# A vision tower on one core: the routed experts' last 64 features as pairs of 64-row matmuls

## The chip, the cores and the metric

The kernel runs on one core of one Trainium2 chip. The metric is the device time of one execution in microseconds (us), as the median of several runs.

## The reference

32 images of 38 tokens with 192 features pass through patch embedding, a selective scan, a layer of routed experts, a two-directional Mamba layer and a second mixture of experts. Each layer adds to a residual. The change lies in the first layer of routed experts alone, which is this, all in float32:

```python
B, S, H, F, E, TOP_K = (4, 512, 192, 768, 8, 2)
router_logits = jnp.einsum('th,eh->te', xf, Wr)
topk_vals, topk_idx = jax.lax.top_k(router_logits, TOP_K)
h = jnp.einsum('th,efh->etf', xf, Wi) + bi[:, None, :]     # wide: 192 -> 768
h = jax.nn.gelu(h, approximate=False)
expert_out = jnp.einsum('etf,ehf->eth', h, Wo) + bo[:, None, :]   # narrow: 768 -> 192
```

## The kernel before

The 32 images go through in four groups of 304 tokens. A first pass (`first`) holds the embedding, the first scan and the routing; a second pass (`part_a`, `part_b`) holds the Mamba scans and the second mixture. Each part has 12 steps, and the order of the work on each engine is written out by hand: five programs with semaphores between them.

The routed experts work on blocks of 128 token rows of one expert. There are 34 blocks, 0 to 33, each with its own expert's weights from DRAM. Blocks 0 to 4 (`SCAN_BLOCKS`) lie between the steps of the last group's first scan. Blocks 5 to 14 lie between the routing steps of the last group, 15 to 25 in the first `part_a`, and 26 to 33 in the first `part_b`, which have no scan yet (`IN_SCAN`, `IN_ROUTE`, `IN_PART_A`, `IN_PART_B`).

A block b passes through these steps:

- SP (`load_block`) fetches its 128 rows into XB, the wide weights into WX and WXR, and the narrow weights into WX and WXB. Three buffers rotate, so the fetches for block b wait for steps of block b - 3.
- `turn(b)` on TensorE (lines 1885 and 1886) transposes the rows: features 0 to 127 and features 64 to 191, into one PSUM bank (`SHARED_BANK`).
- `copy_x(b)` on VectorE (lines 1492 and 1493) copies them to XT: slot 0 holds features 0 to 127; slot 1 holds features 128 to 191 on partitions 64 to 127, and zeros on partitions 0 to 63. Then it signals `xt_copied`.
- `widen(b, halves)` makes the 768 hidden features as six tiles of 128, in two halves of three, each half in a PSUM bank. Each tile is two matmuls: the first 128 features (WX), and the last 64 (WXR, whose upper 64 rows are zeros, so it has 128 rows as well). One float32 matmul of the program is two MATMULs and two LDWEIGHTS in the trace, all on line 1670.
- `gelus(b)` on ScalarE (line 1008) makes HX from each half as it is signalled by `wide_mm`.
- `narrow(b)` multiplies HX by the narrow weights (12 MATMULs) into the same shared bank as the transposes. It waits for `xt_copied` of block b + 2, since VectorE reads that bank.
- `copy_y(b)` (line 1500) adds the bias, and GpSimd stores the rows.

TensorE's order in `experts(b)` from block 5 on is: first half of b, `turn(b + 1)`, second half of b, `narrow(b - 1)`. For blocks 0 to 4 it is `turn(b + 1)`, first half, `narrow(b - 1)`, second half. On VectorE each step ends with `copy_x(b + 1)` and `copy_y(b - 1)`.

The second pass starts behind the last blocks: SP waits for `mixed` of group 1 before it reads the scan's rows (line 510).

Of the kernel before, what the change touches and what calls it, by code (L numbers as in the profile page):

```python
# [6 lines left out]
BATCH, SEQ, D = 32, 38, 192  # L7
# [7 lines left out]
DM, DR = 128, 64  # L15
# [39 lines left out]
SCATTERS = 16 * (2 * TILES + 1)  # L55
M_CHAIN = 17
NBLK = 128

# [56 lines left out]
def vit_tower(nc, x_p, c128a, c64a, c128, c64, ex_m, ex_r, ex_b, out_m, out_r):  # L117
    fp32, bf16, i32, u32 = mybir.dt.float32, mybir.dt.bfloat16, mybir.dt.int32, mybir.dt.uint32
    ALU, ACT, AX = mybir.AluOpType, mybir.ActivationFunctionType, mybir.AxisListType
    with ExitStack() as ctx:  # L120
# [19 lines left out]
        negA = sb("negA", [128, 2 * FEAT_BLOCKS])  # L140

        WX = sb("WX", [128, 3, FFN + FT * D + FT])
        WXR = sb("WXR", [128, 3, FFN])
        WXB = sb("WXB", [128, 3, D])


# [113 lines left out]
        GATHERED = (GA0, GA0, GA, GA)  # L260
        passed = xp[0:TW, :, :].rearrange("p k t -> p (k t)")[:, 6 * D:6 * D + 2 * HALF_BLOCKS * EXPERTS].rearrange("p (a b e) -> p a b e", a=2, e=EXPERTS)
        XTOK = M.ACC
        ZERO = WXR[:, :, :].rearrange("p b n -> p (b n)")[:, 0:PLACES * D // 8]
        LZ = aP[:, 0, 1, :]
        DT24 = aP[0:RANK, 1, 1, 0:T]
        DT24K = aP[:, 1, 1, 0:T]
# [66 lines left out]

        negA_bounded, prep_pool, prep_act = sem("negA_bounded"), sem("prep_pool"), sem("prep_act")
        blank = sem("blank")
        BLANKS = 18

        def norm_signals(s, n, count):
            s.ln_mean, s.ln_var = sig(n + "_ln_mean", count), sig(n + "_ln_var", count)
# [141 lines left out]
        def _(sp):  # L481
# [8 lines left out]
                a, b = SEG64[i], SEG64[i + 1]  # L490
                sp.dma_start(CR[0:DR, a:b], c64[:, a:b]).then_inc(s_const[i], 16)
            sp.wait_ge(prep_pool, 2)
            zeros = slots_d.rearrange("(p j r) n -> p j (r n)", p=128, j=8)

            def write_first_rows(p):

# [22 lines left out]
            def first(s, p, m):  # L519
                if s is not None:  # L520
                    sp.wait_ge(P.rows_written.sem, P.rows_written.after(s, 96))
                for c in range(QSTEPS):
                    if c == 5:
                        if m is not None:
                            sp.wait_ge(scan_out.sem, scan_out.after(m, 1))
                            sp.dma_start(h_md[m], M.Hm[:, :]).then_inc(h_stored.sem, 16)
                            sp.dma_start(h_rd[m], M.Hr[:, :]).then_inc(h_stored.sem, 16)
                    if s is None and p is None and c in (0, 1, 6):
                        load_block(SCAN_BLOCKS + (0, 1, 6).index(c))
                    if c == 5:  # L530
                        if follows(p) is not None:
                            sp.wait_ge(tok_mm.sem, tok_mm.after(p, 2))
                            sp.dma_start(xp[:, :, :], x_p[p + 1]).then_inc(s_x, 16)
                    if c == 9 and p is not None:
                        write_first_rows(p)
                    if s is not None:
                        read_first_rows(s, c)
                    if s == 0 and c >= SLOTS:
                        sp.dma_start(zeros[:, c - SLOTS, :], ZERO).then_inc(s_zero, 16)
                    if s is not None and p is None:  # L540
                        if c == 4:
                            sp.wait_ge(table_ready, 1)
                            sp.wait_ge(c1_ready.sem, c1_ready.after(s, 1))
                            sp.wait_ge(base_ready.sem, base_ready.after(s, 1))
                        if c in (4, 5, 6):
                            load_wide(expert_of(c - 4), c - 4)
                        if c in (7, 8):
                            load_narrow(expert_of(c - 7), c - 7)
                        if c == 9:
                            sp.wait_ge(s_zero, 128)  # L550
                            sp.wait_ge(scattered.sem, scattered.after(PER_HALF, 0))
                        if c in (9, 10, 11):
                            load_rows(place_of(c - 9), c - 9)
                        if c == 11:
                            load_narrow(expert_of(2), 2)
                            load_block(3)
                            load_block(4)
# [6 lines left out]
            def load_wide(expert, p):  # L564

                sp.dma_start(WX[:, p, 0:WI], ex_m[bass.ds(expert, 1), :, 0:WI].rearrange("e p n -> p (e n)")).then_inc(s_wide[p], 16)
                sp.dma_start(WXR[DR:128, p, :], ex_r[bass.ds(expert, 1), :, :].rearrange("e p n -> p (e n)")).then_inc(s_wide[p], 16)

            def load_narrow(expert, p):

# [116 lines left out]
        def _(pool):  # L687
# [36 lines left out]
            def first(s, p, m):  # L724
                pieces = [(t, k) for t in range(TILES) for k in range(2)]
                for c in range(QSTEPS):
                    if s is not None:
                        if s == 0 and c == 0:
                            decay_step(0, 0)
                        if c + 1 < QSTEPS:  # L730
                            decay_step(s, c + 1)
                        elif p is not None:
                            decay_step(p, 0)
                        first_product(s, c)
                    if m and c in (1, 2, 3, 4):
                        scatter(m - 1, *pieces[c + 1])
                    if m and c == 6:
                        scatters_done(m - 1)
                    if m is not None and c == 10:
                        pool.wait_ge(s_zero, 128)  # L740
                        pool.wait_ge(xtok_copied.sem, xtok_copied.after(m, 2))
                        pool.wait_ge(slots_ready.sem, slots_ready.after(m, 1))
                        pool.sem_inc(turn_taken, 1)
                    if m is not None and c in (10, 11):
                        for t, k in (pieces[c - 10:c - 9] if s is not None else pieces if c == 10 else ()):
                            scatter(m, t, k)
                    if s is None and m is not None and c == 10:
                        pool.dma_start(keep_d[m], KEEP[:, :, :].rearrange("p t n -> p (t n)")).then_inc(scattered.sem, 16)
                    b = block_now(s, p, c)
                    if b is not None and b >= SCAN_BLOCKS:  # L750
                        if b == SCAN_BLOCKS:
                            for j in range(SCAN_BLOCKS - 2, SCAN_BLOCKS - 1):
                                store_block(j)
                        store_block(b - 1)
                    elif b is not None and b >= 2:
                        store_block(b - 2)
                if s is not None and m is not None:
                    pool.dma_start(keep_d[m], KEEP[:, :, :].rearrange("p t n -> p (t n)")).then_inc(scattered.sem, 16)
                if s is None and m is not None:
                    scatters_done(m)  # L760
# [381 lines left out]
        def _(dve):  # L1142
            for part in (CRA[DR:128, :], CR[DR:128, :], P.HrK[DR:128, :], P.XrK[DR:128, :], P.SQrK[DR:128, :], HIDrK[DR:128, :],
                         M.HrK[DR:128, :], M.XrK[DR:128, :], Q.SQrK[DR:128, :], M.LWK[:, :], M.gateK[:, :], M.ACCK[:, :],
                         Q.HrK[DR:128, :], Q.XrK[DR:128, :], Q.LWK[:, :], Q.gateK[:, :],
                         XT[0:DR, :, 1, :], HB[:, :]):
                nc.vector.memset(part, 0.0).then_inc(blank, 1)
            dve.wait_ge(blank, BLANKS)

# [337 lines left out]
            def copy_x(b):  # L1487
# [2 lines left out]
                if b >= 3:  # L1490
                    dve.wait_ge(wide_mm.sem, wide_mm.after(b - 3, 2))
                nc.vector.tensor_copy(XT[:, p, 0, :], PS[:, SHARED_BANK, 0:128])  # L1492
                nc.vector.tensor_copy(XT[DR:128, p, 1, :], PS[DR:128, SHARED_BANK, 128:256]).then_inc(xt_copied.sem, 1)  # L1493

            def copy_y(b):
                p = b % 3
# [167 lines left out]
        def _(pe):  # L1664
# [246 lines left out]
                else:  # L1911
                    pe.wait_ge(gelu_ready.sem, gelu_ready.after(HALF_BLOCKS + (q - 3) // 2, (q - 3) % 2 + 1))

            def widen(b, halves):
                p = b % 3
                if 0 in halves:
                    pe.wait_ge(xt_copied.sem, xt_copied.after(b, 1))
                    pe.wait_ge(s_wide[p], 32 * (b // 3) + 32)
                for h in halves:
                    bank_free(b, h)  # L1920
                    for j in range(HALF_FT):
                        out, f = PS[:, wide_bank(b, h), j * 128:(j + 1) * 128], h * HALF_FT + j
                        mm(out, WX[:, p, f * 128:(f + 1) * 128], XT[:, p, 0, :], True, False)
                        last = mm(out, WXR[:, p, f * 128:(f + 1) * 128], XT[:, p, 1, :], False, True)
                    last.then_inc(wide_mm.sem, 1)

            def narrow(b):
                p = b % 3
# [12 lines left out]
            def experts(b):  # L1941
# [3 lines left out]
                    return  # L1945
                if b < SCAN_BLOCKS:
                    turn(b + 1)
                    widen(b, (0,))
                    if b >= 1:
                        narrow(b - 1)  # L1950
                    widen(b, (1,))
                    return
                if b < BLOCKS:
                    widen(b, (0,))
                    if b + 1 < BLOCKS:
                        turn(b + 1)
                    widen(b, (1,))
                narrow(b - 1)

            def first(s, p, m):  # L1960
# [241 lines left out]
def _arrays(inp):  # L2202
# [66 lines left out]
    wo = I["L0_ffn_Wo"].reshape(EXPERTS, D, FT, 128).transpose(0, 3, 2, 1).reshape(EXPERTS, 128, FT * D)  # L2269
    bi = I["L0_ffn_bi"].reshape(EXPERTS, FT, 128).transpose(0, 2, 1)  # L2270
    ex_m = np.ascontiguousarray(np.concatenate([wi[:, 0:DM], bi, wo], axis=2))
    ex_r = np.ascontiguousarray(wi[:, DM:D])
    ex_b = np.ascontiguousarray(I["L0_ffn_bo"].reshape(EXPERTS, 1, D))
    b = "L1_attn_"
    put_both("down", I[b + "down_W"])
# [46 lines left out]
```

## Time and profile before

| | us |
|---|---|
| median of 3 runs | 959.54 |
| lowest and highest | 952.37, 961.0 |
| the profiled execution | 956.27 |
| its span, first to last instruction | 954.5 |

In the profile PE is TensorE's matmul side, PEld its weight loads, DVE is VectorE, ACT is ScalarE, POOL is GpSimd and SP the engine that issues most transfers. The mean granted clock of TensorE is 0.893 of full speed. PE is busy for 740.4 us of the span, DVE for 566.5, ACT for 404.1 and POOL for 394.6.

### The profile page before, as it was taken

Reading aid. Unit: us, or ns where it says so; the run is one execution under the profiler, and the core shown is the slowest. Engines: PE = TensorE matmul, PEld = TensorE weight load, DVE = VectorE, ACT = ScalarE, POOL = GpSimd, SP = SyncE. Lnnn points to the kernel's source line nnn. Section 1 sums busy time; section 2 is a strip of 40 time slices with the busy share of each in tenths; the row PEclk is TensorE's granted clock in tenths of the full one; section 3 lists DMA queues with packets and bytes.
Section 4 is the critical chain, followed back from the end, with each engine's and each line's share of the span. In section 5 each row is a group of like instructions: output and inputs, shape, how many; then the busy total and the mean of one; then the engine's idle time right before and its main releaser. Section 6 shows DMA issues by size and latency. Waiting matters only on the chain. (4 is left out here: it accounts for less than half of the span.)

```text
span 954.5 us, 11504 instructions
## 1 busy us (share of the span) xinstructions
PE 740.4 (78%) x3608; PEld 587.9 (62%) x3608; DVE 566.5 (59%) x968; ACT 404.1 (42%) x876; POOL 394.6 (41%) x311
## 2 busy tenths in 40 slices
PE   7977878586458879997999568777769885986756
PEld 5644656455327869997999356555556664764434
DVE  4167769679766532322112587988777787789320
ACT  1548275374134224332445446373617361733110
POOL 1045745655673311312013344544538333734503
PEclk9899899798678889999999789898979998997977
DMA  9469755355495567798786878697588657866221
GB/s 351 133 208 337 215 152 151 90 134 142 117 273 144 166 182 242 233 281 248 218 244 190 206 194 217 176 224 190 143 229 216 150 156 224 226 165 180 79 72 27
DMA packets 84668, 179.51 MB, mean 188 GB/s; under 512 B 12740, under 2 KB 32832, under 8 KB 83840
## 3 DMA queue, kind: packets, MB, share of 16 engines
q1 hardware_dynamic: 79776, 171.55, 64.1%
q0 software_dynamic: 4832, 7.24, 2.6%
q8 instruction: 28, 0.46, 0.2%
q14 instruction: 32, 0.26, 0.1%
HBM read 158.02 MB, written 20.69 MB: 187 GB/s over the span
## 5 line engine op out<-in xcount | busy, mean ns | idle before, releaser
L1670 PE MATMUL PS<-PR,CM 128*128 128x304 f32 (+1 forms) x672 | 184.1, 415 | 89.4 <-POOL PR L790 60.6
L790 POOL TENSOR_TENSOR PR<-ST,V 128x608 f32<-128x608 f32 x96 | 142.2, 1481 | 185.7 <-DVE ST L1304 160.2
L1670 PEld LDWEIGHTS PS<-PR,CM 128*128 128x128 f32 x672 | 125.7, 219 | 131.6 <-POOL PR L790 74.4
L956 ACT ACTIVATE dA<-dA,negA 128x304 f32<-128x304 f32 x192 | 93.7, 539 | 151.5 <-DMA BB<-rows_d 151.2
L1304 DVE TENSOR_TENSOR_SCAN ST<-dA,PS 128x608 f32<-128x608 f32 x96 | 136.3, 1420 | 15.3 <-ACT dA L956 11.3
L1008 ACT ACTIVATE HID<-PS,WX 128x128 f32<-128x128 f32 x204 | 59.6, 367 | 141.3 <-PE PS L1670 141.2
L703 POOL TENSOR_TENSOR dA<-dA,aP 128x607 f32<-128x607 f32 x48 | 70.7, 1474 | 73.6 <-ACT aP L976 70.8
L1293 DVE TENSOR_TENSOR PS<-BB,PS 128x608 f32<-128x608 f32 x96 | 76.2, 794 | 21.7 <-DMA BB<-rows_d 10.5
L1670 PE MATMUL PS<-XT,WX 128*128 128x128 f32 x408 | 82.5, 285 | 1.0 <-ACT HID L1008 1.0
L1670 PE MATMUL PS<-WX,HID 128*128 128x192 f32 x408 | 76.6, 339 | 8.3 <-DVE XT L1493 8.3
L1670 PE MATMUL PS<-XT,WXR 128*128 128x128 f32 x408 | 81.6, 283 | 0.0
L718 POOL DMA_DIRECT2D outs_d<-xp x34 | 19.2, 564 | 140.8 <-DVE xp L1500 140.7
L1670 PEld LDWEIGHTS PS<-WX,HID 128*128 128x128 f32 x408 | 69.6, 199 | 9.3 <-issue 5.1
L709 POOL TENSOR_TENSOR PR<-PR,ST 128x608 f32<-128x608 f32 x32 | 47.2, 1474 | 58.3 <-DVE ST L1283 58.2
L1283 DVE TENSOR_TENSOR_SCAN ST<-dA,PS 128x608 f32<-128x608 f32 x48 | 67.8, 1412 | 3.2 <-POOL dA L703 1.8
L1500 DVE TENSOR_TENSOR xp<-PS,WXB 128x192 f32<-128x192 f32 x34 | 12.2, 357 | 96.2 <-PE PS L1670 96.2
L1670 PEld LDWEIGHTS PS<-XT,WX 128*128 128x128 f32 x408 | 67.1, 202 | 2.2 <-ACT HID L1008 1.2
L1670 PE MATMUL PS<-WX,CM 128*128 128x304 f32 x192 | 57.0, 438 | 11.7 <-POOL WX L798 11.4
L1670 PEld LDWEIGHTS PS<-XT,WXR 128*128 128x128 f32 x408 | 64.7, 200 | 0.0
L1670 PEld LDWEIGHTS PS<-WX,CM 128*128 128x128 f32 x192 | 37.4, 198 | 27.6 <-POOL WX L798 14.9
L1670 PE MATMUL PS<-HB,CM 96*128 96x152 f32 (+1 forms) x240 | 49.5, 358 | 0.0
L1492 DVE COPY XT<-PS 128x128 f32<-128x128 f32 x34 | 9.8, 289 | 63.5 <-PE PS L1886 52.3
(363 smaller groups left out, 1318.7 us busy)
## 6 DMA issues: line engine op xcount, KB each, us to landing
dA<-rows_d SPq DMA_DIRECT2D x144, 304.0 KB, 4.4
BB<-rows_d SPq DMA_DIRECT2D x144, 304.0 KB, 4.9
WX<-ex_m SPq DMA_DIRECT2D x34, 576.0 KB, 3.9
WX<-ex_m SPq DMA_DIRECT2D x34, 387.0 KB, 3.8
slots_d<-WXR SPq DMA_DIRECT2D x8, 960.0 KB, 8.0
WXR<-ex_r SPq DMA_DIRECT2D x34, 192.0 KB, 4.6
WX<-gates_d SPq DMA_DIRECT2D x4, 1216.0 KB, 6.4
CM<-c SPq DMA_DIRECT2D x1, 4430.0 KB, 19.6
```

The source lines that it names most:

```text
L703: nc.gpsimd.tensor_tensor(now[:, 1:], now[:, 1:], before[:, 0:QB * T - 1], ALU.mult).then_inc(ap_ready.sem, 1)
L709: nc.gpsimd.tensor_tensor(PR3[c % 3], PR3[c % 3], STq[:, c % 2], ALU.mult).then_inc(P.product.sem, 1)
L718: pool.dma_start(outs_d[b // HALF_BLOCKS][at:at + 128, :], YB[:, b % 3, :]).then_inc(out_rows[b % 3], 16)
L790: nc.gpsimd.tensor_tensor(PRq[:, c % 2], STq[:, c % 2], DIRS[k].Cw.unsqueeze(1).broadcast_to([128, QB, T]), ALU.mult).then_inc(q_product.s ...
L956: last = nc.scalar.activation(dAq[:, slot, i, :], dAq[:, slot, i, :], ACT.Exp, scale=negA[:, j:j + 1])
L1008: last = nc.scalar.activation(HX[:, p, f, :], PS[:, wide_bank(b, h), j * 128:(j + 1) * 128], ACT.Gelu, bias=WX[:, p, FFN + f:FFN + f + 1])
L1283: nc.vector.tensor_tensor_scan(flat(STq[:, c % 2], False), flat(dAq[:, slot], False), BP[0], 0.0, ALU.mult, ALU.add).then_inc(P.scanned.se ...
L1293: nc.vector.tensor_tensor(BPq[k], BBq[:, slot], BW[k].unsqueeze(1).broadcast_to([128, QB, T]), ALU.mult).then_inc(b_times_w.sem, 1)
L1304: nc.vector.tensor_tensor_scan(flat(STq[:, c % 2], back), flat(dAq[:, slot], back), BP[k][:, ::-1] if back else BP[k], 0.0, ALU.mult, ALU. ...
L1492: nc.vector.tensor_copy(XT[:, p, 0, :], PS[:, SHARED_BANK, 0:128])
L1500: nc.vector.tensor_tensor(YB[:, p, :], PS[:, SHARED_BANK, 256:256 + D], WXB[:, p, :], ALU.add).then_inc(y_copied.sem, 1)
L1670: return nc.tensor.matmul(out, lhsT, rhs, start=first, stop=last)
```

## The change

The last 64 features of a hidden tile are multiplied with 64 rows of the array instead of 128. The weights of the first three tiles (half 0) now lie on partitions 0 to 63 of WXR and those of the last three (half 1) on partitions 64 to 127; slot 1 of XT holds the last 64 features on both halves of the partitions, for which `copy_x` gets a third copy. WXR is half as wide. From block 5 on, the main parts of both halves come first, then `turn(b + 1)`, then the 64-row matmuls of both halves in turn (tile j of half 0, tile j of half 1), then `narrow(b - 1)`. In blocks 0 to 4 each half stays by itself: its three main parts, then its three 64-row matmuls.

Beside that, the zeros that SP writes to `slots_d` come from a WXR that is too small for eight transfers of 960 KB, and so go as sixteen of half the size; GpSimd clears half as much of WXR; and VectorE doesn't clear slot 1 of XT.

```diff
         WX = sb("WX", [128, 3, FFN + FT * D + FT])
-        WXR = sb("WXR", [128, 3, FFN])
+        WXR = sb("WXR", [128, 3, FFN // 2])
...
-        ZERO = WXR[:, :, :].rearrange("p b n -> p (b n)")[:, 0:PLACES * D // 8]
+        ZERO = WXR[:, :, :].rearrange("p b n -> p (b n)")[:, 0:PLACES * D // ZEROS]
...
                     if s == 0 and c >= SLOTS:
-                        sp.dma_start(zeros[:, c - SLOTS, :], ZERO).then_inc(s_zero, 16)
+                        for j in range(2):
+                            sp.dma_start(zeros[:, 2 * (c - SLOTS) + j, :], ZERO).then_inc(s_zero, 16)
...
-                sp.dma_start(WXR[DR:128, p, :], ex_r[bass.ds(expert, 1), :, :].rearrange("e p n -> p (e n)")).then_inc(s_wide[p], 16)
+                sp.dma_start(WXR[:, p, :], ex_r[bass.ds(expert, 1), :, :].rearrange("e p n -> p (e n)")).then_inc(s_wide[p], 16)
...
                 nc.vector.tensor_copy(XT[:, p, 0, :], PS[:, SHARED_BANK, 0:128])
-                nc.vector.tensor_copy(XT[DR:128, p, 1, :], PS[DR:128, SHARED_BANK, 128:256]).then_inc(xt_copied.sem, 1)
+                nc.vector.tensor_copy(XT[DR:128, p, 1, :], PS[DR:128, SHARED_BANK, 128:256])
+                nc.vector.tensor_copy(XT[0:DR, p, 1, :], PS[DR:128, SHARED_BANK, 128:256]).then_inc(xt_copied.sem, 1)
...
-            def widen(b, halves):
+            def wide_out(b, h, j):
+                return PS[:, wide_bank(b, h), j * 128:(j + 1) * 128]
+
+            def wide_main(b, h):
+
                 p = b % 3
-                if 0 in halves:
+                if h == 0:
                     pe.wait_ge(xt_copied.sem, xt_copied.after(b, 1))
                     pe.wait_ge(s_wide[p], 32 * (b // 3) + 32)
-                for h in halves:
-                    bank_free(b, h)
-                    for j in range(HALF_FT):
-                        out, f = PS[:, wide_bank(b, h), j * 128:(j + 1) * 128], h * HALF_FT + j
-                        mm(out, WX[:, p, f * 128:(f + 1) * 128], XT[:, p, 0, :], True, False)
-                        last = mm(out, WXR[:, p, f * 128:(f + 1) * 128], XT[:, p, 1, :], False, True)
-                    last.then_inc(wide_mm.sem, 1)
+                bank_free(b, h)
+                for j in range(HALF_FT):
+                    f = h * HALF_FT + j
+                    mm(wide_out(b, h, j), WX[:, p, f * 128:(f + 1) * 128], XT[:, p, 0, :], j == 0, False)
+
+            def wide_rest(b, halves):
+
+                p = b % 3
+                for j in range(HALF_FT):
+                    for h in halves:
+                        rows = slice(h * DR, (h + 1) * DR)
+                        last = mm(wide_out(b, h, j), WXR[rows, p, j * 128:(j + 1) * 128], XT[rows, p, 1, :], False, j == HALF_FT - 1)
+                        if j == HALF_FT - 1:
+                            last.then_inc(wide_mm.sem, 1)
...
                     turn(b + 1)
-                    widen(b, (0,))
+                    wide_main(b, 0)
+                    wide_rest(b, (0,))
                     if b >= 1:
                         narrow(b - 1)
-                    widen(b, (1,))
+                    wide_main(b, 1)
+                    wide_rest(b, (1,))
                     return
                 if b < BLOCKS:
-                    widen(b, (0,))
+                    wide_main(b, 0)
+                    wide_main(b, 1)
                     if b + 1 < BLOCKS:
                         turn(b + 1)
-                    widen(b, (1,))
+                    wide_rest(b, (0, 1))
                 narrow(b - 1)
```

## Rows read from the trace of the kernel before

**Rows 1.** The page, part 2: the span in 40 slices of 23.9 us.

```profile
PE   7977878586458879997999568777769885986756
DMA  9469755355495567798786878697588657866221
```

**Rows 2.** The chain that ended last: start, duration, what.

```profile
527.95 0.34 DVE m_ACC L1543
...
528.91 4.35 DMA BB<-rows_d
```

**Rows 3.** Busy time of each engine by stretch, then clock, DMA share, GB/s.

```profile
346.50:402.00 55.50, 52.16 (x372) 50.89 (x373) 16.55 (x71) 22.68 (x63) 15.07 (x18) 0.93 0.80 244
402.00:442.00 40.00, 35.84 (x276) 34.89 (x275) 7.86 (x30) 12.25 (x43) 10.58 (x13) 1.00 0.97 276
442.00:528.00 86.00, 82.55 (x575) 78.22 (x575) 19.50 (x63) 35.83 (x97) 14.44 (x20) 0.98 0.71 212
```

**Rows 4.** Timeline of PE and ACT in block 16: start, duration, work, count.

```profile
405.32 0.27 PE L1886 MATMUL PS<-CM,xp 128*128 128x128 f32 x1
405.43 0.39 PE L1670 MATMUL PS<-XT,WX 128*128 128x128 f32 x2
405.65 0.39 PE L1670 MATMUL PS<-XT,WXR 128*128 128x128 f32 x2
...
406.77 2.13 PE L1670 MATMUL PS<-WX,HID 128*128 128x192 f32 x12
408.74 0.38 PE L1670 MATMUL PS<-XT,WX 128*128 128x128 f32 x2
...
405.49 0.88 ACT L1008 ACTIVATE HID<-PS,WX 128x128 f32<-128x128 f32 x3 [3.38 <-PE PS L1670]
```

**Rows 5.** Timeline of DVE in the same block.

```profile
405.69 0.29 DVE L1492 COPY XT<-PS 128x128 f32<-128x128 f32 x1 [1.16 <-issue]
405.99 0.29 DVE L1493 COPY XT<-PS 64x128 f32<-64x128 f32 x1
```

**Rows 6.** Who waited for whom, 346 to 528 us: total us, times, longest.

```profile
PE PS L1885 <- DMA xp<-slots_d: 9.2, 5, 5.1
...
PE PS L1670 <- DVE XT L1493: 3.3, 3, 1.9
```

**Rows 7.** Timeline of DVE and PE where narrow waited for the copy.

```profile
393.99 0.29 DVE L1493 COPY XT<-PS 64x128 f32<-64x128 f32 x1
...
394.43 1.90 PE L1670 MATMUL PS<-WX,HID 128*128 128x192 f32 x6 [1.89 <-DVE XT L1493]
```

**Rows 8.** Timeline of weight loads: 128 columns each, behind matmuls of one column.

```profile
402.98 0.42 PEld L1670 LDWEIGHTS PS<-fold,CM 96*128 96x128 f32 x3
...
403.32 0.30 PEld L1670 LDWEIGHTS PS<-CM,ones_d 128*128 128x128 f32 x2
```

**Rows 9.** Timeline of PE and DVE from block 2 to block 6.

```profile
317.80 0.63 PE L1670 MATMUL PS<-XT,WX 128*128 128x128 f32 x2
...
327.25 0.43 PE L1670 MATMUL PS<-XT,WX 128*128 128x128 f32 x2
...
337.84 2.19 PE L1670 MATMUL PS<-WX,HID 128*128 128x192 f32 x12 [1.80 <-DVE XT L1493]
...
346.50 0.47 PE L1885 MATMUL PS<-CM,xp 128*128 128x128 f32 x1 [5.13 <-DMA xp<-slots_d]
...
330.81 0.36 DVE L1500 TENSOR_TENSOR xp<-PS,WXB 128x192 f32<-128x192 f32 x1 [2.38 <-PE PS L1670]
...
337.40 0.29 DVE L1493 COPY XT<-PS 64x128 f32<-64x128 f32 x1
```

**Rows 10.** The stretch of blocks 0 to 4, columns as in Rows 3.

```profile
290.00:332.00 42.00, 35.22 (x235) 34.22 (x235) 22.74 (x59) 15.87 (x38) 16.35 (x14) 0.85 0.53 157
```

**Rows 11.** Transfers: KB each and us to landing; one issue of zeros on SP.

```profile
WXR<-ex_r SPq DMA_DIRECT2D x34, 192.0 KB, 4.6
...
86.55 0.59 SPq L539 DMA_DIRECT2D slots_d<-WXR  x1
```

More of the change, by code:

```diff
@@ L57 @@
 NBLK = 128
+ZEROS = 16
 def _layout(widths):
@@ L335, in vit_tower @@
         blank = sem("blank")
-        BLANKS = 18
+        BLANKS = 17
         def norm_signals(s, n, count):
@@ L492, in _ @@
             sp.wait_ge(prep_pool, 2)
-            zeros = slots_d.rearrange("(p j r) n -> p j (r n)", p=128, j=8)
+            zeros = slots_d.rearrange("(p j r) n -> p j (r n)", p=128, j=ZEROS)
             def write_first_rows(p):
@@ L549, in first @@
                         if c == 9:
-                            sp.wait_ge(s_zero, 128)
+                            sp.wait_ge(s_zero, 16 * ZEROS)
                             sp.wait_ge(scattered.sem, scattered.after(PER_HALF, 0))
@@ L739, in first @@
                     if m is not None and c == 10:
-                        pool.wait_ge(s_zero, 128)
+                        pool.wait_ge(s_zero, 16 * ZEROS)
                         pool.wait_ge(xtok_copied.sem, xtok_copied.after(m, 2))
@@ L1145, in _ @@
                          Q.HrK[DR:128, :], Q.XrK[DR:128, :], Q.LWK[:, :], Q.gateK[:, :],
-                         XT[0:DR, :, 1, :], HB[:, :]):
+                         HB[:, :]):
                 nc.vector.memset(part, 0.0).then_inc(blank, 1)
@@ L2271, in _arrays @@
     ex_m = np.ascontiguousarray(np.concatenate([wi[:, 0:DM], bi, wo], axis=2))
-    ex_r = np.ascontiguousarray(wi[:, DM:D])
+    ex_r = np.ascontiguousarray(np.concatenate([wi[:, DM:D, 0:FFN // 2], wi[:, DM:D, FFN // 2:]], axis=1))
     ex_b = np.ascontiguousarray(I["L0_ffn_bo"].reshape(EXPERTS, 1, D))
```

## The prediction

> **What bounds the kernel now.** I read the page's slices first, then the chain of waits, then the busy times by stretch, and last the timelines of TensorE and VectorE inside one block. The blocks run from 290 to 526 us. In the slices between 330 and 530 us TensorE stands at 7 to 9 tenths, and the transfers are high in the same place [rows 1]. The chain of waits starts in the middle of the kernel: its first piece is VectorE's `m_ACC` at 527.95 us, and then SP's first read of the second pass lands [rows 2]. That `m_ACC` stands in VectorE's order behind the last `copy_y`, so all that the blocks take is paid by the end of the kernel, one for one; and behind 528 us the change touches nothing.
>
> Which engine sets a block's time differs by stretch. From 442 to 528 us PE is busy 82.55 of 86 us, from 346.5 to 402 us 52.16 of 55.5; there TensorE's own order is the bound. From 402 to 442 us the transfers are, with a share of 0.97 at 276 GB/s [rows 3], and TensorE waits for token rows at `turn`: 9.2 us in five waits, of which 5.1 are the one at 346.5 us, so 4.1 fall in the later stretch [rows 6, 9]. By its loads this stretch has seven blocks, 15 to 21. The 27 blocks from 7 on are then 20 that TensorE sets and 7 that the transfers set.
>
> One block in the timeline [rows 4]: the second transpose starts at 405.32 us, six pairs of wide MATMULs follow from 405.43, `narrow` starts at 406.77 and ends its stream at 408.74, where the next block's first half starts. A MATMUL of 128 columns comes every 0.11 us (two between 405.43 and 405.65), and lasts 0.27 us from start to end. The first half before the transposes is as long as the second, 1.33 us; so the block is 1.33 + 0.22 + 1.33 + 1.97, that is 4.85 us.
>
> **The third copy.** This edit has a firm price, and it decides most of the rest. The first copy starts 0.37 us behind the second transpose (405.69 against 405.32), the second 0.30 us later, and it ends at 406.28 [rows 5]. Where `narrow` waited for it, the matmul started 0.15 us behind the copy's end (394.43 against 394.28) [rows 7]. So VectorE lets `narrow` go 0.96 + 0.15 = 1.11 us behind the transpose's start, while TensorE gets there at 1.45 us: 0.34 us of cover. A third copy of 0.30 us (the source and size of the second) moves VectorE's release to 1.41 us. As long as TensorE takes 1.45 us this is hidden; once it is faster, the copy is what is late next. The most that a block can gain is 1.45 - 1.41 = 0.04 us. In three blocks VectorE is late already [rows 6]; there the third copy costs its 0.30 us in full, 0.9 us in all. The same holds at 337.84 us [rows 9]: another 0.3.
>
> **The pairs.** TensorE keeps the number of instructions: 12 MATMULs and 12 weight loads for the last 64 features of a block. If two that lie on different row halves run at once, the 12 take about 6.5 places of 0.11 us, 0.72 us instead of 1.33. The trace has no 64-row operation, so the price lies between 0.72 and 1.33 us. What speaks for the upper end: weight loads of 128 columns behind matmuls of one column still come every 0.11 us (three from 402.98 to 403.32) [rows 8]. Loads alone fill the place that a matmul has now, so a pair gains only if its loads overlap too. The Trainium skill (TensorE: Matmul & The Clock Gate, "LDWEIGHTS (loading the stationary operand)") puts a load at its columns divided by 1.2 GHz whatever its rows, which is 0.107 us here; these rows agree with 0.11. By that rule alone the 12 loads would take 1.3 us and a pair would gain nothing, unless the loads of two row groups overlap, which the same page's part on packing and the Trainium skill's TensorEngine Tiling ("Key Properties") say they can. I take the overlap for a little more likely than not.
>
> **The switch between 128 and 64 rows.** No row shows it. The lower end is nothing: the stream goes on as before. The upper end is that the array runs empty and the next load is exposed: a MATMUL lasts 0.27 us and the next starts after 0.11, so 0.16 us must run out, and a load adds 0.11, together 0.27 us [rows 4, 8]. I take 0.16, the row that an array running empty has to show at least; two switches, in and out, are 0.33 us per stretch of 64-row work. A gain has no reason. The Trainium skill (TensorEngine Tiling, "Key Properties") says that a change of tiling mode drains the engine; it gives no time.
>
> With both, TensorE reaches `narrow` at 0.11 + 0.72 + 0.33 = 1.16 us behind the transpose (1.37 with the dear switch), earlier than VectorE's 1.41 in either case. So from block 7 on a block is paid at 1.41 instead of 1.45: 17 blocks by -0.04 is -0.7 us, and the three late ones +0.9.
>
> **Blocks 0 to 6.** In blocks 0 to 4 no half has a partner, so nothing overlaps, and each of ten halves pays two switches. From 317.80 to 330.81 us TensorE runs without a gap up to the `copy_y` behind which VectorE's long fold of weights starts; from there the way goes over the copy at 337.40, `narrow` at 337.84, the residual and SP's store to the late token rows at 346.5 us [rows 9]. Four halves lie on it for certain (block 2's second, block 3's two, block 4's first, the one at 327.25), the other six only in part, since PE is busy 35 of 42 us there [rows 10]. I take six: 6 x 0.33 = 2.0 us; the ends are 0 and 10 x 0.54 = 5.4. What blocks 5 and 6 do of themselves falls into the wait of 5.13 us at 346.5 us.
>
> **The rest.** The order of the main parts costs nothing: `turn` still stands 1.33 us into the block. ScalarE now gets both halves at the end of the 64-row part, three activations of 0.88 us at a time [rows 4]; the first user of that bank or of HX is at least a `narrow` of 1.97 us plus a main part of 0.67 later, so 1.8 us of activations stay covered, for three banks as well as for four. SP's wide load waits for that signal, but two buffers ahead. WXR's 192 KB become 128 rows of half the length [rows 11]. In the seven blocks that transfers set, this may cost up to 0.1 us each, an estimate of mine from WXR being a seventh of a block's 1.3 MB; nothing elsewhere. Eight more issues of zeros, 0.59 us each on SP's queue [rows 11], lie in the first group's scan, where SP waits for the scan anyway. The shorter clearing at the start is hidden by the first loads.
>
> **The sum.** -0.7 + 0.9 + 0.3 + 2.0 = +2.5 us; with the ends of the switches and the transfers it runs from about 0 (-0.7 + 0.9 + 0.3) to +6.6. The profiled execution took 956.27 us, 3.3 below the median of the runs, so it would be 958.8 against it; against the median, 959.54 + 2.5 = 962.
>
> **Rivals.** First: the pairs don't overlap, and the switch is paid. Then TensorE reaches `narrow` at 0.11 + 1.33 + 0.33 = 1.77 us, up to 1.98 with the dear switch: 0.32 to 0.53 us later than now in the 17 blocks that TensorE sets, 5.4 to 9.0 us. The seven blocks between 402 and 442 us would have 2.2 to 3.7 us more work, within the 4.1 us that TensorE waits there, so they cost nothing. With 1.2 for the third copy and 2.0 to 5.4 for the scan's halves it is +8.6 to +15.6, in the middle +12: 971. Its point is whether loads of two row halves run at once; the loads every 0.11 us speak for it [rows 8]. Slower. Second: neither overlap nor switch, the change doesn't do what it says. Then TensorE stays at 1.45 us, the copy is covered, and +1.2 remain: 961. Third: the gain arrives because what frees `narrow` isn't the copy but something earlier, or VectorE starts its copy sooner than 0.37 us behind the transpose. Then a block gains up to 1.45 - 0.83 = 0.62 us, 17 x 0.62 is 10.5, less 1.2: about 950. The wait in the code and the three late blocks speak against it [rows 6, 7].
>
> **Chances.** The forecast has 0.47, the first rival 0.31, the second 0.15, the third 0.07. This kernel's measurement can tell about 1% (9.6 us) from no change. The first rival lies above it in some seven cases of ten and the forecast hardly ever; the third lies at it. So slower by over 1%: 0.24; faster: 0.05; within: 0.71. The range reaches up to the first rival's 975, and down to 954 for the spread of 9 us that three runs of the kernel before show.
>
> **What would show it.** In the profile after: three copies to XT per block, and `narrow` starting 0.15 us behind the third in nearly every block, with a new wait of PE on VectorE that has some 25 entries of 0.1 to 0.3 us. The 12 MATMULs from XT and WXR start in pairs, within 0.8 us (overlap) or over 1.33 us (none). A gap of 0.16 us or more stands before the first 64-row MATMUL and before the first 128-row one behind it. A block takes 4.8 us. The first late token rows come at about 348.5 us, and the chain's `m_ACC` at about 530.5. Wrong would be: blocks of 4.3 us (the copy doesn't bind), blocks above 5.1 us (no overlap), or a clock below the 0.93 to 1.00 of now in those stretches.

## The result and the profile after

| | before | after |
|---|---|---|
| median, us | 956.05 (20 runs) | 961.08 (20 runs) |
| lowest and highest | 949.04, 964.86 | 955.22, 964.86 |
| the profiled execution | 956.27 | 964.67 |
| its span | 954.5 | 962.7 |

The ratio is 1.0047, with a 95% interval of 1.0027 to 1.0067: +4.5 us, between 2.6 and 6.4. The forecast was +2.5 us, which lies just below that interval, and no change by the bound of 1%, which came true. More runs of the kernel before moved its median from 959.54 to 956.05, so +2.5 meant 958.6 on the new scale, and 961.08 came. The profiled execution of after lies 3.6 us above its own median, that of before 0.2; of the 8 us between the two spans only about five are the change.

Where the time went is seen by cutting both timelines at the same two places. The transposes of block 7 wait for late token rows in both; before at 346.50 us [rows 9], after at 351.05. VectorE's `m_ACC` is where the chain of waits starts; before at 527.95 [rows 2], after at 536.24. Behind it the second pass takes 426.5 us in both. So in this pair of profiles 4.6 us arise before block 7 and 3.7 in blocks 7 to 33. The kernel after even comes earlier to block 0 (second transpose at 283.59 against 286.01), so from there to block 7's second transpose it takes 67.73 us where it was 60.75. The chain of waits of the kernel after, its first piece:

```profile
536.24 0.34 DVE m_ACC L1546
```

A plain block in the timeline of TensorE after, which answers to [rows 4]:

```profile
403.52 1.50 PE L1673 MATMUL PS<-XT,WX 128*128 128x128 f32 x12
404.86 0.27 PE L1888 MATMUL PS<-CM,xp 128*128 128x128 f32 x1
404.96 0.27 PE L1889 MATMUL PS<-CM,xp 128*128 128x128 f32 x1
405.17 0.94 PE L1673 MATMUL PS<-XT,WXR 64*128 64x128 f32 x12
406.32 2.19 PE L1673 MATMUL PS<-WX,HID 128*128 128x192 f32 x12 [0.22 <-DVE XT L1496]
```

and the same block in VectorE's timeline, which answers to [rows 5]:

```profile
405.27 0.29 DVE L1494 COPY XT<-PS 128x128 f32<-128x128 f32 x1 [1.20 <-PE PS L1889]
405.58 0.29 DVE L1495 COPY XT<-PS 64x128 f32<-64x128 f32 x1
405.89 0.29 DVE L1496 COPY XT<-PS 64x128 f32<-64x128 f32 x1
```

A place in a timeline is named by the block whose transposes stand in it; the wide matmuls around them are those of the block before. "Behind the transposes" counts from the start of the second one.

The pairs overlap: the 12 matmuls of 64 rows end 0.94 us after the first starts, and since one lasts 0.27, their starts lie within 0.67 us, where they took 1.22. The timeline of weight loads shows four of them within 0.30 us, so the loads of the two row halves overlap as well:

```profile
405.17 0.30 PEld L1673 LDWEIGHTS PS<-XT,WXR 64*128 64x128 f32 x4 [0.17 <-issue]
```

And the gain doesn't arrive. The third copy ends at 406.18, `narrow` starts 0.14 us later, 1.36 behind the second transpose instead of 1.45. Its stream takes 2.03 to 2.06 us instead of 1.97, so the plain block goes from 4.86 to 4.84 us. Who waited for whom from 346 to 540 us, which answers to [rows 6]:

```profile
PE PS L1673 <- DVE XT L1496: 10.8, 24, 2.7
...
PE PS L1888 <- DMA xp<-slots_d: 8.5, 6, 4.9
```

The wait for the copy has grown from 3 entries to 24; in 20 of them it is 0.22 to 0.28 us, and the other four are the places where VectorE is late. The waits for token rows have hardly changed.

In blocks 0 to 4 the price of switching between 128 and 64 rows is seen. Block 3's first half after (the six matmuls that start at 326.84 open its second half):

```profile
323.14 0.83 PE L1673 MATMUL PS<-XT,WX 128*128 128x128 f32 x6
323.91 0.93 PE L1673 MATMUL PS<-XT,WXR 64*128 64x128 f32 x6
324.77 2.23 PE L1673 MATMUL PS<-WX,HID 128*128 128x192 f32 x12
326.84 0.83 PE L1673 MATMUL PS<-XT,WX 128*128 128x128 f32 x6
```

Six main matmuls occupy 0.77 us up to the first of 64 rows and not 0.67; those take 0.86 instead of 0.67, and `narrow` behind them 2.07 instead of 1.97. Each of the two switches costs 0.09 us before the first matmul and 0.10 before the second, 0.39 together. Between the transposes of blocks 4 and 5 and of 5 and 6 lie 6.66 and 8.01 us, where it was 5.94 and 7.29.

### The profile page after: what moved, and what is told of

Same layout as the page of the kernel before. It is cut to its first block and busy times, and to the rows that moved or that the text cites. A ratio compares the mean times of both kernels' runs of the same rounds, so it can differ in the third digit from the quotient of the medians.

```text
span 962.7 us, 11545 instructions
## 1 busy us (share of the span) xinstructions
PE 741.5 (77%) x3608; PEld 578.1 (60%) x3608; DVE 576.9 (60%) x1001; ACT 401.4 (42%) x876; POOL 393.4 (41%) x311
## 5 line engine op out<-in xcount | busy, mean ns | idle before, releaser
L1010 ACT ACTIVATE HID<-PS,WX 128x128 f32<-128x128 f32 x204 | 56.8, 373 | 153.9 <-PE PS L1673 153.8
L1673 PE MATMUL PS<-WX,HID 128*128 128x192 f32 x408 | 84.6, 362 | 15.4 <-DVE XT L1496 15.4
L1673 PEld LDWEIGHTS PS<-WX,HID 128*128 128x128 f32 x408 | 74.7, 211 | 20.9 <-issue 13.7
L1673 PE MATMUL PS<-XT,WX 128*128 128x128 f32 x408 | 56.3, 289 | 1.0 <-ACT HID L1010 1.0
L1673 PEld LDWEIGHTS PS<-XT,WX 128*128 128x128 f32 x408 | 54.5, 205 | 2.1 <-ACT HID L1010 1.2
L1673 PEld LDWEIGHTS PS<-HB,CM 96*128 96x128 f32 x240 | 40.8, 207 | 8.2 <-issue 2.6
L1673 PE MATMUL PS<-p_Xm,WX 128*128 128x304 f32 x88 | 33.5, 465 | 14.5 <-ACT HID L903 11.6
```

The costliest lines, as they stand in the source:

```text
L1010: last = nc.scalar.activation(HX[:, p, f, :], PS[:, wide_bank(b, h), j * 128:(j + 1) * 128], ACT.Gelu, bias=WX[:, p, FFN + f:FFN + f + 1])
L1673: return nc.tensor.matmul(out, lhsT, rhs, start=first, stop=last)
```

## The experiments

Ratios are to the kernel before, timed in the same rounds; differences against the changed kernel or between experiments come from two such ratios, and so are uncertain by some 4 us. "Narrow at" is the start of `narrow` behind the start of the second transpose, a block is the distance of two transposes.

**e1_copy: the third copy alone, in the kernel before.**

```diff
-                nc.vector.tensor_copy(XT[DR:128, p, 1, :], PS[DR:128, SHARED_BANK, 128:256]).then_inc(xt_copied.sem, 1)
+                nc.vector.tensor_copy(XT[DR:128, p, 1, :], PS[DR:128, SHARED_BANK, 128:256])
+                nc.vector.tensor_copy(XT[0:DR, p, 1, :], PS[DR:128, SHARED_BANK, 128:256]).then_inc(xt_copied.sem, 1)
```

> The kernel before with the third copy to XT alone (its 64 rows meet the zero rows of WXR, so the result stays). Theory: the copy has 0.34 us of cover in a plain block, so narrow still starts 1.45 us behind the transposes there and a block stays 4.86 us; only where VectorE was late already it costs 0.3 us each, together about +1.2 us. Rival (the third copy alone carries the whole loss): +5 us, with narrow waiting in most blocks.

Ratio 0.9979 (0.9945 to 1.0013), that is -2 us, from -5 to +1; neither +5 nor a loss of 2 is left, and +1.2 is just within. The timelines in block 17 show the copy under cover; it runs from 411.09 to 411.38, and `narrow` starts without a wait at 1.45:

```profile
410.17 0.27 PE L1887 MATMUL PS<-CM,xp 128*128 128x128 f32 x1
...
411.62 0.66 PE L1671 MATMUL PS<-WX,HID 128*128 128x192 f32 x3
```

The copy itself in VectorE's timeline:

```profile
411.09 0.29 DVE L1494 COPY XT<-PS 64x128 f32<-64x128 f32 x1
```

In the blocks in which VectorE is late, `narrow` is at 2.89, 2.40 and 3.81 us where it was 2.58, 2.09 and 3.50: 0.31 each, as said. From block 7's transposes to block 33's it is 166.4 us against 166.2, so in this pair of profiles the waits for token rows behind them took most of these 0.9 us up. By itself the copy isn't the loss.

**e2_free: the changed kernel, with the third copy off the way of `narrow`.**

```diff
-                nc.vector.tensor_copy(XT[DR:128, p, 1, :], PS[DR:128, SHARED_BANK, 128:256])
-                nc.vector.tensor_copy(XT[0:DR, p, 1, :], PS[DR:128, SHARED_BANK, 128:256]).then_inc(xt_copied.sem, 1)
+                nc.vector.tensor_copy(XT[DR:128, p, 1, :], PS[DR:128, SHARED_BANK, 128:256]).then_inc(xt_copied.sem, 1)
+                dve.wait_ge(xt_copied.sem, xt_copied.after(b, 1))
+                nc.vector.tensor_copy(XT[0:DR, p, 1, :], XT[DR:128, p, 1, :]).then_inc(xt_doubled.sem, 1)
...
+                if 0 in halves:
+                    pe.wait_ge(xt_doubled.sem, xt_doubled.after(b, 1))
```

> The changed kernel, but the third copy reads XT instead of PSUM and has its own signal for the 64-row matmuls, so narrow goes behind the second copy. Theory (the third copy is what caps the gain): narrow starts about 1.1 us behind the transposes instead of 1.36, a plain block takes 4.6 instead of 4.84 us, 17 such blocks give -4 us or a little more against the changed kernel, back to the time of the kernel before or slightly below. Rival (the cap is TensorE's own, the switch out of 64 rows): narrow stays at 1.36, time unchanged.

Ratio 0.9992 (0.9961 to 1.0023); against the changed kernel's 1.0047 that is -5 us, from -9 to -2. TensorE's timeline in block 29:

```profile
488.84 0.27 PE L1890 MATMUL PS<-CM,xp 128*128 128x128 f32 x1
488.95 0.27 PE L1891 MATMUL PS<-CM,xp 128*128 128x128 f32 x1
489.15 0.94 PE L1675 MATMUL PS<-XT,WXR 64*128 64x128 f32 x12
490.02 0.76 PE L1675 MATMUL PS<-WX,HID 128*128 128x192 f32 x3
```

`narrow` is at 1.07, with no wait in front, and plain blocks take 4.58 us, as expected. The copy from XT takes 0.22 us instead of 0.29 in 29 of the 34 blocks; where it takes longer, GpSimd is at work (last section). So the copy caps the gain of the pairs at 0.02 us a block; the pairs themselves are worth 0.28, with both switches paid. 17 such blocks are 4.4 us. The interval alone would leave a smaller saving open; the blocks in the timeline don't.

**e3_scan128: the changed kernel, with blocks 0 to 4 in 128 rows again.** XT gets a third slot, so that one holds x over zeros and one zeros over x; the pairs use the filled halves of both.

```diff
-        XT = sb("XT", [128, 3, 2, 128])
+        XT = sb("XT", [128, 3, 3, 128])
...
-                nc.vector.tensor_copy(XT[DR:128, p, 1, :], PS[DR:128, SHARED_BANK, 128:256])
+                nc.vector.tensor_copy(XT[DR:128, p, 2, :], PS[DR:128, SHARED_BANK, 128:256])
...
-                        rows = slice(h * DR, (h + 1) * DR)
-                        last = mm(wide_out(b, h, j), WXR[rows, p, j * 128:(j + 1) * 128], XT[rows, p, 1, :], False, j == HALF_FT - 1)
+                        rows = slice(h * DR, (h + 1) * DR) if b >= SCAN_BLOCKS else slice(0, 128)
+                        last = mm(wide_out(b, h, j), WXR[rows, p, j * 128:(j + 1) * 128], XT[rows, p, 1 + h, :], False, j == HALF_FT - 1)
```

> The changed kernel, but blocks 0 to 4 multiply the last 64 features with all 128 rows again (x and zeros in two slots of XT); the pairs from block 5 on stay. Theory: each of the ten halves gives back 0.29 us (1.62 against 1.33 in the profile after), of which six to ten lie on the path: -2 to -3 us against the changed kernel. Rival (the loss before 346 us is the clock's phase in that profile, and not the halves): within 1 us of the changed kernel.

Ratio 0.9999 (0.9966 to 1.0032): -4.6 us against the changed kernel, more than the 2 to 3 expected, but the two intervals leave anything from -8 to -1. The timeline of block 3's second half has no switch left:

```profile
324.15 0.83 PE L1673 MATMUL PS<-XT,WX 128*128 128x128 f32 x6
324.81 0.83 PE L1673 MATMUL PS<-XT,WXR 128*128 128x128 f32 x6
325.48 1.20 PE L1673 MATMUL PS<-PR,CM 128*128 128x152 f32 x8
```

It takes 1.33 us, where with 64 rows it is 1.62 up to the next work and 0.10 more inside that. The expectation counted the first part only, 0.29 for each half; with 0.39 ten halves are 3.9 us. Whether all of the 4.6 are switches isn't shown, since this version also has less slow clock than the changed kernel (what stays open, below).

**e4_serial: the changed kernel, with the 64-row matmuls half by half.**

```diff
-                for j in range(HALF_FT):
-                    for h in halves:
+                for h in halves:
+                    for j in range(HALF_FT):
```

> The changed kernel, but the 64-row matmuls go by half (three tiles of half 0, then three of half 1) instead of in turn. Theory (the gain of the pairs comes from two matmuls on different row halves at a time): the 12 take 12 x 0.132 = 1.6 us instead of 0.67, narrow starts 1.9 us behind the transposes, +0.5 us in each of 17 to 20 blocks, +9 us against the changed kernel. Rival (a 64-row matmul is itself cheaper, whatever its neighbour): narrow stays at 1.36 us, no change.

Ratio 1.0091 (1.0051 to 1.0130): +4 us against the changed kernel, from 0 to +8, where +9 was expected. A miss of mine, twice. Only the first gap behind a switch is 0.21 us, the rest are 0.11, so 0.132 was a mean over a switch. And the order of the program doesn't forbid all overlap, as the timeline of block 17 shows:

```profile
417.14 0.27 PE L1889 MATMUL PS<-CM,xp 128*128 128x128 f32 x1
417.34 1.26 PE L1673 MATMUL PS<-XT,WXR 64*128 64x128 f32 x12
418.53 2.23 PE L1673 MATMUL PS<-WX,HID 128*128 128x192 f32 x12
```

The 12 starts lie within 0.99 us: more than 0.67, less than 1.3. Eleven weight loads are done in 0.96 us in the view of loads. The single records have half 1's first matmul at 417.67 us, ahead of half 0's fourth at 417.78. The records don't name the rows; I tell the halves apart by length, since the matmul at 417.67 lasts 0.37 us, as in the pairs only the first of each half does, and 0.27 is that of the others. `narrow` is at 1.39, without a wait: now TensorE binds, 0.03 us beyond the copy, and a plain block takes 4.91 us. Over 17 plain blocks that is 1.2 us; what the rest of the +4 is, if it isn't the spread of the runs, stays open. The rival, a 64-row matmul that is cheaper by itself, is out: within one half they come every 0.11 us behind the first gap, as often as those of 128 rows, and so do the six of block 3's first half in the changed kernel.

**e5_order: the kernel before, with the new order alone from block 5 on**, in 128 rows and with two copies.

```diff
+            def widen_main(b):
...
+            def widen_rest(b):
...
-                    widen(b, (0,))
+                    widen_main(b)
                     if b + 1 < BLOCKS:
                         turn(b + 1)
-                    widen(b, (1,))
+                    widen_rest(b)
```

> The kernel before with the new order alone from block 5 on (main parts of both halves, transposes, the last 64 features of both halves), all with 128 rows and two copies. Theory: a plain block stays 4.86 us with narrow at 1.45, but ScalarE gets both halves late, so its root and then VectorE's scaling at the start of part b are late, narrow and the projection behind it wait about 0.6 us each, and block 28 comes 9.2 instead of 8.2 us behind 27: +1 to +1.5 us in all. Rival (the order costs nothing, as the prediction had it): block 28 at 8.2, 0 us.

Ratio 1.0032 (1.0002 to 1.0061), +3 us, from 0 to 6. Plain blocks stay at 4.86 with `narrow` at 1.45, and block 28 comes 9.53 us behind block 27, where it was 8.19. ScalarE's and TensorE's timelines show why:

```profile
475.90 1.28 ACT L1008 ACT_TABLE_LOAD   x1 [0.86 <-PE PS L1670]
477.20 1.66 ACT L1008 ACTIVATE HID<-PS,WX 128x128 f32<-128x128 f32 x6
478.71 0.56 ACT L1110 ACTIVATE HB<-m_Xm,CM 96x304 f32<-96x304 f32 x1
```

```profile
479.33 3.34 PE L1670 MATMUL PS<-HB,CM 96*128 96x304 f32 x14 [0.94 <-ACT HB L1110]
```

ScalarE can't start block 26's activations until both halves are done, and HB stands behind them in its order; the projection needs HB. The order costs something by itself. The interval reaches down to 0, so beyond the 1.3 us at this place the size stays open.

**e6_free_scan128: both costs out**, the edits of e2_free and e3_scan128 together.

> The changed kernel with both of its costs taken out: the third copy reads XT and doesn't hold narrow, and blocks 0 to 4 use 128 rows. Theory (the two are independent costs): the gains add, plain blocks 4.58 us and no switches before block 5, so some 9 us below the changed kernel and 4 us below the kernel before, ratio 0.995 to 0.998. Rival (both only moved the same slack, at the token rows' arrival): no better than either alone, ratio 1.000.

Ratio 0.9946 (0.9923 to 0.9969), 951.4 us: -5.2 us against before and -9.7 against the changed kernel. The two add, as far as the intervals can tell. This version beats both kernels.

**e7_act_first: as e6, with HB ahead of block 26's activations on ScalarE.**

```diff
-                    if nxt is not None and n == 1:
+                    if nxt is not None and n == (0 if nxt == 0 else 1):
                         act.wait_ge(L.ln_x.sem, L.ln_x.after(nxt, 1))
```

> As the run with both costs taken out, but ScalarE makes HB for the first group ahead of block 26's activations instead of behind them. Theory: the projection no longer waits for ScalarE, 0.6 us less between blocks 27 and 28, and the total about 0.6 us below that run. Rival: VectorE's late scaling now holds ScalarE and the activations move by as much, no gain.

Ratio 0.9955 (0.9930 to 0.9979), which the timing can't tell from e6. In the timeline the projection no longer waits for HB; block 28 comes 8.33 us behind block 27 instead of 9.27, 0.9 and not 0.6:

```profile
471.71 1.46 PE L1675 MATMUL PS<-WX,HID 128*128 128x192 f32 x8
473.01 3.24 PE L1675 MATMUL PS<-HB,CM 96*128 96x304 f32 x14
```

**e8_switches: as e2, with one more pair of switches per block from block 5 on.** The last main tile of half 1 moves behind the first pair.

```diff
-                for j in range(HALF_FT):
+                for j in range(HALF_FT - late):
...
                 for j in range(HALF_FT):
+                    if late and j == 1:
+                        f = FT - 1
+                        mm(wide_out(b, 1, 2), WX[:, p, f * 128:(f + 1) * 128], XT[:, p, 0, :], False, False)
...
-                    wide_main(b, 1)
+                    wide_main(b, 1, True)
...
-                    wide_rest(b, (0, 1))
+                    wide_rest(b, (0, 1), True)
```

> The changed kernel with the third copy from XT and its own signal, and one more pair of switches per block from block 5 on: the last main tile of half 1 goes between the first pair of 64-row matmuls and the other two. Theory (a pair of switches costs 0.39 us, as the starts in the profile after show): a plain block 4.97 instead of 4.58 us, and +8 to +10 us against the same kernel without the extra switches. Rival (a switch costs only the 0.09 us seen before the first 64-row matmul): 4.7 us, +3 us.

Ratio 1.0134 (1.0100 to 1.0168): +13.6 us against e2, more than expected, since 29 blocks of 0.39 us make 11.3 at most; the intervals of the two leave 9 to 18. A plain block takes 4.97 us, 0.39 more to the hundredth. Its timeline:

```profile
415.82 0.27 PE L1891 MATMUL PS<-CM,xp 128*128 128x128 f32 x1
416.02 0.49 PE L1675 MATMUL PS<-XT,WXR 64*128 64x128 f32 x4
416.44 0.49 PE L1675 MATMUL PS<-XT,WX 128*128 128x128 f32 x2
416.86 0.72 PE L1675 MATMUL PS<-XT,WXR 64*128 64x128 f32 x8
```

Two matmuls of 128 rows between switches occupy 0.42 us, where they occupy 0.22 elsewhere.

## Why the prediction was right, and where a step wasn't

- **The blocks set the end, one for one.** Right: 527.95 to 954.5 and 536.24 to 962.7 are both 426.5 us. In the profiles of the experiments the same stretch takes 425.1 to 429.3 us, so it holds to within 3 us of one execution.
- **The third copy caps the gain.** Right in mechanism; that the size fits is in part luck. `narrow` was put at 1.41 us behind the transposes and came at 1.36, since the copy started 0.31 us behind the transpose, as in most blocks, and not 0.37 as in the one that I took. By that alone a block would have gained 0.09 us and not the 0.04 that I gave as the most. But `narrow`'s stream behind the pairs takes 2.03 to 2.06 us instead of 1.97, which the sum left out, and 0.02 remained. e2 shows that the copy is the cap, e1 that it costs little while TensorE is slow.
- **The pairs overlap.** I put 0.72 us and a little over even odds; it took 0.67 between the first and the last start. The doubt came from loads every 0.11 us [rows 8], which holds for loads into the same rows. The trace after decides that loads into different row halves run together, and here the Trainium skill's "Different tiles can execute LdWeights and Matmul in parallel" (TensorEngine Tiling, "Key Properties") agrees with it.
- **The switch.** Taken as 0.33 us a pair, 0.16 each way, from how long a matmul outlasts the next one's start; it is 0.39, within the ends. The size is near, the form isn't: the gap of 0.16 us or more that was to stand before the first matmul in the new mode is 0.09, and another 0.10 stands behind it. By the records the next matmul starts 0.07 us before the last one ends (0.27 against 0.20), so the array emptying before it isn't what they show; the ends of matmuls in these profiles are modelled, which leaves that open.
- **Blocks 0 to 6.** "I take six" of ten halves, 2.0 us, was too small: with 0.39 for all ten it is 3.9, and e3 gave back 4.6, e6 against e2 some 4.4, each uncertain by about 4. The profile after shows 1.4 us for the four halves between blocks 4 and 6 alone. Probably part of what was idle in [rows 10] was no cover: `narrow` waits 3.2 us there for VectorE's copy, and VectorE has itself waited 3.6 us for TensorE's output at 305.16 us before.
- **"The rest. The order of the main parts costs nothing."** This step failed. I followed who reuses the banks and HX, and not what is queued behind the activations on ScalarE. Blocks 27 to 28 went from 8.19 to 9.26 us. e5 shows that the order alone does it, e7 that the place of HB on ScalarE is the cause of 0.9 of these 1.1 us.
- **Transfers.** At most 0.1 us in each of seven blocks was allowed for WXR. Its transfers landed in 4.0 us in the median instead of 4.6, so nothing shows.

The terms as measured are -0.02 x 17 = -0.3 for plain blocks, up to +1.2 for copies where VectorE was late, +1.1 for the order, and +3.9 for the switches of blocks 0 to 4: +5.9 us at most, as some of it meets waits, against 4.5 (2.6 to 6.4). The forecast's sum had the right sign and the right places for the copy and the switches; the term of the switches was half of what it is (2.0 for 3.9), and that of the order was put at nothing for 1.1. The measured terms come to 3.4 us more than the forecast; that the result is only 2 us above it is no merit of the sum. Of the rivals, no overlap is out by the profile after; the change does what it says, which takes out the second; and the third, an early release, isn't there, since 24 waits end with the third copy.

One sign of being wrong, as the prediction lists them, did come: a clock below the 0.93 to 1.00 of before. What stays open: the profile of after holds more slow clock than that of before. The granted clock from 286 us to block 7's transposes is 0.76 against 0.84, from 402 to 442 us 0.90 against 1.00 [rows 3]. From block 2's transposes to block 3's it took 12.5 us instead of 8.6, with matmuls at the lower level from 299 to 307 us. The same stretch took 9.4 in e2 and e4 and 12.3 in e8, all with the same work up to there, so this length varies between executions, and it prices the clock. In the changed kernel and e8 some 9 us of the stretch are at the lower level, in e2 and e4 2.6: 6 us more of it cost 3 us. From block 7's transposes on, the largest part of the 3.7 us lies in blocks 15 to 22 (42.4 us instead of 40.1), where the clock was lower and one wait for token rows 2.1 us long.

No experiment aimed at whether 64-row matmuls make slow clock likelier, but the mean granted clock of every run is on record, and these say more than the profiles. With 64 rows in blocks 0 to 4 it is 0.887 for the changed kernel (20 runs), 0.888 for e2, 0.886 for e4 and 0.885 for e8. With 128 rows there it is 0.892 to 0.894 for the kernel before, 0.894 for e1, 0.893 for e3, 0.894 for e5 and 0.890 for e6 and e7; each mean is uncertain by 0.001 to 0.002. Between the changed kernel and e3 that is by my estimate, with the lower level at half speed, some 12 us more of it in each execution. So a part of the 4.5 us, and of what e3 gave back, may be slower clock in place of, or beside, the switches. The timelines show 0.39 us a pair at full clock; how the loss divides between the two isn't shown.

## What to carry to other kernels

Before speeding up one engine's part, work out when each wait behind it would be met if that engine were free: here 0.34 us of cover on VectorE was used up by one added copy, and the 0.28 us per block that the pairs save with their switches paid shrank to 0.02. A half-array matmul pays only in pairs on both row halves, and a stretch of them has to be worth more than two switches (0.39 us), so leave the places that have no partner in full rows. When work is moved on one engine, read on the engines that consume it what stands behind the consumer, not only who waits for its buffers.

## What the runs showed of the hardware that I hadn't expected

- Matmuls on different row halves overlap even if the program doesn't alternate them: with six on one half and then six on the other, the seventh started 0.11 us before the fourth (halves told apart by the length of the records), and the 12 took 0.99 us between the first and last start (0.67 when alternated, 1.22 in 128 rows).
- A switch between 128 and 64 rows costs 0.19 us each way, in two parts: 0.09 before the first matmul in the new mode and 0.10 before the second. Doubling the switches gave 0.39 us per block again.
- A 64-row copy of 128 float32 columns took 0.22 us from SBUF and 0.29 from PSUM on VectorE, though both moved rows 64 to 127 to rows 0 to 63.
- The copy from SBUF can be held up by GpSimd, the one from PSUM wasn't. In the profiles of e2, e6, e7 and e8 it took 1.17 to 1.23 us in two or three blocks each, and each time it ended 0.08 to 0.09 us behind a GpSimd TENSOR_TENSOR that was running when it started. The copy from PSUM just before ran beside the same instruction in 0.29 us. All its other long cases (0.26 to 0.50 us) overlap GpSimd work as well. The timeline of e2:

```profile
328.94 1.46 POOL L712 TENSOR_TENSOR V<-V,ST 128x608 f32<-128x608 f32 x1 [3.96 <-DVE ST L1286]
328.99 0.29 DVE L1496 COPY XT<-PS 64x128 f32<-64x128 f32 x1
...
329.31 1.17 DVE L1498 COPY XT<-XT 64x128 f32<-64x128 f32 x1
```
